# A decoder layer whose ternary feed-forward weights are made in the first batch instead of before the feed-forward

## The reference

```python
x = x + attn(layernorm(x))                  # 16 heads of 32, rotary, causal; w_qkv, w_o
x = x + ssm(ctx, z=layernorm(x))            # state-space scan, 16 states for each of 512 channels
x = x + ffn(layernorm(x))                   # below

def ternarize_weights(w):
    gamma = mean(abs(w))                    # one number for the whole matrix
    return sign(round(w / (gamma + EPS))) * gamma
def bitlinear(x, w):                        # forward value
    return einsum(absmax_quant(layer_norm(x)), ternarize_weights(w))
ffn = bitlinear(gelu(bitlinear(x, w_fc)), w_proj)     # 512 -> 2048 -> 512
```

## Time and profile before

| | us |
|---|---|
| median of 3 runs (lowest, highest) | 1058.46 (1055.85, 1059.35) |
| the profiled execution's own time | 1058.11 |
| its span | 1056.3 |
| PE busy | 949.3 |
| DVE busy | 853.2 |
| ACT busy | 764.9 |
| POOL busy | 616.9 |

### The profile page before, as it was taken

How to read it: one execution, slowest core, us unless ns; L and a number is a source line. 1 busy time by engine, 2 the same in 40 slices (tenths; PEclk the granted TensorE clock), 3 DMA queues, 4 the chain that set the end, 5 groups by cost and what they waited for, 6 DMA issues and landing times.

```text
span 1056.3 us, 18159 instructions
## 1 busy us (share of the span) xinstructions
PE 949.3 (90%) x5848; PEld 641.1 (61%) x5848; DVE 853.2 (81%) x1151; ACT 764.9 (72%) x1478; POOL 616.9 (58%) x439
## 2 busy tenths in 40 slices
PE   6989998899988999979889997667889999999997
PEld 5466666668755567765555876556755555555544
DVE  5797878986999987898999686998998889885431
ACT  4776867646787775677898669958279989996431
POOL 1387496555545778444658872345667768985410
PEclk9999999999999999978999998989989999999999
DMA  5356265265326544342336555224325565646553
GB/s 168 101 171 187 84 188 172 86 193 155 116 81 217 159 140 136 110 131 60 110 111 205 194 169 192 61 90 138 97 71 116 110 125 120 120 95 140 99 93 69
DMA packets 142812, 136.84 MB, mean 130 GB/s; under 512 B 92336, under 2 KB 96688, under 8 KB 141696
## 3 DMA queue, kind: packets, MB, share of 16 engines
q1 hardware_dynamic: 142720, 135.68, 46.1%
HBM read 90.42 MB, written 24.25 MB: 109 GB/s over the span
## 4 chain that ended last, share of the span: by engine, by line
PE 57%; DVE 20%; issue 9%; ACT 7%; POOL 4%; DMA 2%; SPq 0%; DVEq 0%; ACTq 0%; POOLq 0%
PE ps L1679 10%; PE ps L1748 8%; PE ps L1805 8%; PE ps L1795 8%; DVE hb L1825 6%; PE ps L1692 5%; PE ps L1760 5%; DVE y_acc L1847 4%; PE ps L1722 4%; DVE m_col L1922 2%; PE ps L1734 2%; POOL hb L1295 2%; ACT p_q L1526 2%; PE ps L1622 2%; DVE du L1879 1%
## 5 line engine op out<-in xcount | busy, mean ns | idle before, releaser
L1295 POOL TENSOR_TENSOR hb<-du,b_bc 128x1024 f32<-128x1024 f32 (+1 forms) x160 | 311.5, 1967 | 160.3 <-PE ps L1748 146.6
L1825 DVE TENSOR_TENSOR_SCAN hb<-ps,hb 128x1024 f32<-128x1024 f32 (+1 forms) x128 | 257.2, 2013 | 15.9 <-ACT ps L1415 13.5
L1415 ACT ACTIVATE ps<-delta,a_neg 128x511 f32<-128x511 f32 (+2 forms) x320 | 179.2, 597 | 72.6 <-DVE hb L1825 71.3
L1847 DVE SCALAR_TENSOR_TENSOR y_acc<-ps,ct,y_acc 128x512 f32<-128x512 f32 x256 | 182.0, 742 | 39.0 <-PE ps L1748 38.3
L1748 PE MATMUL ps<-ident,hb 128*128 128x128 f32 x1088 | 157.1, 288 | 35.1 <-DVE hb L1825 15.5
L1748 PEld LDWEIGHTS ps<-ident,hb 128*128 128x128 f32 x1088 | 129.5, 148 | 66.1 <-issue 17.8
L1526 ACT ACTIVATE p_q<-ps,m_col 128x512 f32<-128x512 f32 (+3 forms) x256 | 131.6, 530 | 26.4 <-DVE m_col L1922 22.0
L1795 PE MATMUL ps<-t_fc,xt 128*128 128x512 f16 x512 | 119.4, 387 | 3.3 <-DMA xt<-xs 3.3
L1679 PE MATMUL ps<-xn_t,w_ring 128*128 128x512 f32 x256 | 118.7, 608 | 2.2 <-DVE y_acc L1969 1.0
L1805 PE MATMUL ps<-t_pr,ht 128*128 128x512 f16 x512 | 114.7, 383 | 3.7 <-DMA ht<-hs 3.3
L1542 ACT ACTIVATE p_t<-ps 128x512 f32<-128x512 f32 x160 | 86.5, 603 | 30.6 <-PE ps L1722 30.2
(11 more groups left out here) (141 smaller groups left out, 1559.5 us busy)
## 6 DMA issues: line engine op xcount, KB each, us to landing
w_ring<-in_w_attn SPq DMA_DIRECT2D x32, 512.0 KB, 3.7
qk_d<-hl SPq DMA_DIRECT2D x64, 256.0 KB
q_st<-qk_d SPq DMA_DIRECT2D x128, 128.0 KB, 2.9
...
k_st<-qk_d SPq DMA_DIRECT2D x128, 64.0 KB, 2.3
...
raw_fc<-in_w_fc SPq DMA_DIRECT2D x4, 1024.0 KB, 9.5
```

The lines of the kernel that those rows point to most:

```text
L1295: nc.gpsimd.tensor_tensor(piece_of(e, hi, lo).rearrange("p (a n) -> p a n", a=2), du[b % 2][:, 2 * h:2 * h + 2, lo:hi], b_bc[:, i % BC_RIN ...
L1415: ins = nc.scalar.activation(factors(j, hi, lo)[:, (hi - lo) * m + start:(hi - lo) * (m + 1)], delta[b % 2][:, et, lo + start:hi], ACT.Exp ...
L1825: v.tensor_tensor_scan(h, d, h, 0.0, ALU.mult, ALU.add).then_inc(scan_done, 1)
L1847: v.scalar_tensor_tensor(out=y, in0=bank(kind, r, tb), scalar=ct[:, b % 2, tb, n:n + 1], in1=y, op0=ALU.mult, op1=ALU.add).then_inc(y_free ...
```

## The change

Four things change. The ternary weights are made from the start of the program on, in pieces of 1024 columns through a ring of two: 16 pieces are loaded and summed on ACT, then the same 16 are loaded again, compared on DVE, and stored as float16 in device memory (`t_d`). When the last batch's projections are over, two DMAs load them into `t_fc` and `t_pr`. The ring lies in the second half of `y_acc`, and the comparison's outputs over `gate`, so the second batch's first sum waits for all 16 comparisons and the first `gate` for all stores. The buffers of the feed-forward are laid out anew: `h_sb` lies over the attention's q and k and waits only for the last scores. `XF`, the ring of feed-forward inputs, goes from 7 to 5. And the tables of wished times are replaced by one entry for each state, slot and tile, with new weights, new durations in `follows()`, and `PATIENCE` 0.18 for 0.3.

```diff
-XF = 7
+XF = 5
+RAW = 1024
+RAWS = KD * FF // RAW
+SUMS = 2 * RAWS
-PATIENCE = 0.3
+PATIENCE = 0.18
-STATE = {'exp': [-3.1, 2.9], 'dbu': [-19.1, -2.9], 'scan': [0, 6], 'ht': [7.6, 8.8, 10, 11.2]}
+WEIGHTS = {'fwload': [-82.44, -84.05, -41.76, -59.47, -57.03, -35.38, -62.34, -32.59, -22.52, -61.3, 25.5, -20.65, -24.85,
...
     elif kind == "fwload":
-        w, n = a
-        yield "sp", 6, [act("v", B - 1, 1, 1), sp("lo", B - 1, 3), pool("delta", B - 1, ET - 1)] if w == 0 else \
-            [pe("s", SLOTS - 1, 4) if n < 2 else (act("exp", 2 * DS * (B - 1) - 1), pool("dbu", 2 * DS * (B - 1) - 1))[n - 2]]
+        k, = a
+        yield "sp", 3.0, [act("wsum", k - 2) if k - 2 < SUMS else dve("tern", k - 2 - SUMS)] if k >= 2 else []
...
-        yield "dve", 0.8, [pe(*item)] + ([act("e", p - 1, n)] if p else [])
+        yield "dve", 0.66 if n in (1, 4) else 0.6, [pe(*item)] + ([act("e", p - 1, n)] if p else [])
...
-        yield "act", 1.3, [dve("s", *a)] + ([pe("t", a[0] - 1, 4)] if a[0] else [])
+        yield "act", 0.67 if n in (0, 3) else 0.91, [dve("s", *a)] + ([pe("t", a[0] - 1, 4)] if a[0] else [])
...
     elif kind == "tern":
-        w, n = a
-        yield "dve", 3.7, [dve("wtot", w)]
+        k, = a
+        yield "dve", 1.85, [dve("wtot", k // RAWS), sp("fwload", SUMS + k), dve("delta", 0, ET - 1)] + ([sp("tstore", k - 2)] if k >= 2 else [])
...
+            us *= slow.get(engine, 1.0)
...
-            over[engine, item] = at + us + 0.2
+            over[engine, item] = at + us + settle[engine]
...
+        base[0] = stack_at
+        h_sb = sb("h_sb", [P, 2, FF])
...
+        base[0] = y_acc_at + 4 * LT * DM
+        raw = sb("raw", [P, 2, RAW])
+        base[0] = gate_at
+        low = sb("low", [P, 2, RAW], BF16)
+        tern = sb("tern", [P, 2, RAW], F16)
...
                 elif kind == "fwload":
+                    k, = a
+                    w, c = divmod(k % SUMS, RAWS)
+                    if k >= 2:
+                        if k - 2 < SUMS:
+                            sp.wait_ge(wsum_ready, k - 1)
+                        else:
+                            sp.wait_ge(tern_done, k - 1 - SUMS)
+                    sp.dma_start(raw[:, k % 2, :], t_in[("w_fc", "w_pr")[w]][:, RAW * c:RAW * c + RAW])\
+                        .then_inc(raw_in[k % 2], 16)
+                elif kind == "tstore":
+                    k, = a
+                    w, c = divmod(k, RAWS)
+                    sp.wait_ge(tern_done, k + 1)
+                    sp.dma_start(t_d[w, :, RAW * c:RAW * c + RAW], tern[:, k % 2, :]).then_inc(t_stored[k % 2], 16)
...
                 elif kind == "tern":
+                    k, = a
+                    w = k // RAWS
+                    if k == 0:
+                        delta_made(dve, 0, ET - 1)
+                    if k >= 2:
+                        dve.wait_ge(t_stored[k % 2], 16 * (k // 2))
+                    dve.wait_ge(raw_in[k % 2], 16 * ((SUMS + k) // 2 + 1))
+                    v.tensor_scalar(low[:, k % 2, :], raw[:, k % 2, :], nthr[:, w:w + 1], None, ALU.is_lt).then_inc(is_low, 1)
+                    dve.wait_ge(is_low, k + 1)
+                    v.scalar_tensor_tensor(out=tern[:, k % 2, :], in0=raw[:, k % 2, :], scalar=thr[:, w:w + 1],
+                                           in1=low[:, k % 2, :], op0=ALU.is_gt, op1=ALU.subtract).then_inc(tern_done, 1)
```

More of the change, by code:

```diff
@@ L323 @@
-PACE = {'slot': 18.4, 'ffn': 597.2, 'tile': 15.5, 'tail': 822.6, 'tail_step': 13.6, 'tail_load': -18.7}
+WEIGHT = {'pe': {'ln1b': 1.9,
+        'inproj': -9.5,
+        'xproj': 2.0,
+        'ct': 9.0,
+        'dt': 0.5,
+        'rot': 2.0,
+        'v': 20.2,
+        's': 5.5,
+        't': 3.0,
+        'pv': 61.8,
+        'rz': -4.7,
+        'wo': 17.2,
+        'ht': -2.9,
+        'gt': 4.0,
+        'wtot': 70.8,
+        'xt': 60.6,
+        'fc': -16.2,
+        'ht_ffn': -21.9,
+        'proj': 2.4},
+ 'act': {'carry': -7.8,
+         'exp': -2.8,
+         'skip': -16.1,
+         'ht': -31.6,
+         'ln1b': 47.1,
+         'inproj': -34.1,
+         'silu': 24.7,
+         'xproj': -35.9,
+         'ct': -36.2,
+         'dt': 20.5,
+         'hi': -3.2,
+         'v': 41.1,
+         'e': 1.7,
+         't': -6.7,
+         'pv': 9.8,
+         'rz': -1.0,
+         'gate': -20.6,
+         'xt': -9.7,
+         'ht_ffn': -15.4,
+         'fc': 0.5,
+         'wsum': -23.8,
+         'hn': -21.1},
+ 'dve': {'scan': 0.1,
+         'ht': 7.1,
+         'ln1a': 10.9,
+         'ln1b': 12.1,
+         'inproj': 19.4,
+         'delta': -9.0,
+         'rot': -28.5,
+         's': 0.1,
+         'rz': -9.2,
+         'pv': -28.5,
+         'wo': -4.7,
+         'ln2a': 17.7,
+         'ln2b': 30.4,
+         'gt': -0.9,
+         'wtot': -13.4,
+         'tern': -7.8,
+         'xa': 25.0,
+         'xc': -3.8,
+         'xt': -8.9,
+         'ht_ffn': -19.6,
+         'fc': -23.6,
+         'hstat': 19.2,
+         'hn': 0.9,
+         'hq': -18.5,
+         'proj': -11.1},
+ 'pool': {'delta': 22.8,
+          'dbu': 0.6,
+          'du': -4.9,
+          'lo': 13.3,
+          'xadd': -27.3,
+          'ln1a': -11.3,
+          'ln2a': 2.0,
+          'xa': 5.0,
+          'xc': 15.2,
+          'hstat': -19.7},
+ 'sp': {'xload': 9.4,
+        'cload': 17.5,
+        'wload': -8.9,
+        'lo': -17.3,
+        'xproj': -45.1,
+        'bcload': 18.0,
+        'stack': -10.5,
+        'resid': -24.2,
+        'x2store': 0.6,
+        'fwload': 24.6,
+        'fxload': -27.2,
+        'proj': -13.0}}
@@ L326, in schedule @@
+TILE = {'fxload': [-66.44],
+ 'xa': [-69.82],
+ 'xc': [-40.92],
+ 'xt': [-35.82],
+ 'fc': [-9.26, -30.81, -10.14, -14.5],
+ 'hstat': [-77.43],
+ 'hn': [16.74, 6.58],
+ 'ht_ffn': [-12.97, -15.2],
+ 'proj': [18.32]}
+FIRST_TILE = {'xa': [17.57], 'xc': [-19.46]}
+SWITCH = 17.35
+PATIENCE = 0.18
 def schedule():
@@ L1233, in _ @@
                         sp.wait_ge(hl_stored, 64 * 4 * B)
[L1234 to L1239 removed]
+                    for n in range(2):
+                        sp.wait_ge(t_stored[n], 16 * (w + 1) * RAWS // 2)
+                    dst = (t_fc, t_pr)[w][:].rearrange("p a n -> p (a n)")
+                    sp.dma_start(dst, t_d[w]).then_inc(tw_in[w], 16)
                 elif kind == "fxload":
@@ L1784, in _ @@
                     w, = a
[L1785 to L1786 removed]
+                    pe.wait_ge(wsum_ready, RAWS * (w + 1))
+                    nc.tensor.matmul(bank(kind, *a)[:, 0:RAWS], ones[:], w_sum[:, w, :], start=True, stop=True)\
                         .then_inc(y_full, 1)
```

623 lines of the change are left out of this document (272 added, 351 removed), and 9 rows, old and new, of tables (ATTN_END, SKIP).

## The result

| | before | after |
|---|---|---|
| median (lowest, highest), us | 1058.9 (1055.85, 1060.19) | 1005.28 (1004.94, 1006.11) |
| span of the profiled execution | 1056.3 | 1004.2 |
| first `fc` matmul | 766.7 | 731.3 |
| from the first `fc` to the last scan transposes | 190 | 211.5 |
| from the last scan transposes to the end | 99 | 61.4 |

What follows compares the result with a forecast made beforehand. DVE was taken to bound the kernel up to the first `fc`, PE and ACT up to the last scan transposes, PE and the last tile's chain after: 734 + 208 + 67 = 1009 us of span, 1011 us timed; range 984 to 1046.

Steps and rivals of the forecast that it cites:

- First `fc` at 734: Start to first `fc` matmul: 53 us, then 612.5 us of DVE work at a chosen 0.90; 734 against 767.
- Contention, 7 us: Comparisons in the first batches: running beside POOL lengthens them, adding 7 us of DVE work; bounds 0 and 34.
- rival 2: Comparisons: POOL and DVE block each other in all 16, 34 in place of 7 us of DVE; 1041 us, chance 0.08.
- Both are places where DVE has work waiting. So moving them gains no DVE time by itself: Ahead of first `fc`: comparisons move from 656.6 us and later into the first batches, without DVE gain by itself.
- DVE sets the pace: Up to first `fc`: DVE, busy 621.5 of 714 us (0.87) after the first 53, limits; PE's 0.88 is partly fills.
- The rate rises because fills are fewer and durations nearer to the trace: Ahead of first `fc`: DVE's rate goes above 0.87, to 0.90; fills fall from 399 to 209, planner durations match the trace.
- Stretch 2: First `fc` to last scan transposes: PE 201.5 and ACT 195.3 us of work; 208 us (203 to 214), 17 longer.
- Stretch 3: Last scan transposes to the end: PE work 58.1, idle 6.5 kept, 2.5 added; 67 us (64 to 74) against 98.3.
- The two new waits: Tail: possible waits at the last two tiles' first multiplications, 12 us after the gate, and the last `proj`; 2.5 us added.
- Rival 3: Weight reloads through SP: each of 16 comparisons waits 4.3 us, DVE loses 69 us; 1080 us, chance 0.07.
- The granted clock: Whole kernel: stays at or above the present 0.94 in every stretch although 372 fills go, because matmuls stand closer.
- rival 4: No change: DVE stays at 0.87 before first `fc`, PE's share falls to 0.87 after it; 1058 us, chance 0.05.

## Why the prediction was right, and where its reasons were not

The forecast was 1011 us, the time 1005. The sum was right stretch by stretch in the work that it counted. What carried the gain ahead of the first `fc` was DVE's rate, and that was not derived: 0.90 was taken as the middle between 0.87 and 0.93. Four kernels with the same early weights ran at 0.80 to 0.91, so that it came to 0.911 here was in part luck.

- **First `fc` at 734; it came at 731.** The sum held: DVE's work ahead of the mark was 30.4 + 617.9 = 648.3 us against 645.5 (comparisons 40.9 against 36, the rest 607.4 against 609.6), and the rate 0.911 against the chosen 0.90.
- **Contention, 7 us.** The comparisons took 40.9 us against 29 + 7; above their shortest forms they lost 9.9, and the two shortest halves of a piece cost 0.27 us more than the piece whole, 2 us for the eight. The mechanism was right, and the size near. The rule of the Trainium skill that was weighed there (SBUF — State Buffer, "SBUF: two separate sides": a lock held for the whole instruction) agrees in that single instructions are long; as a price for every step beside POOL, these rows don't bear it out. Waits in all 16 (rival 2, 34 us) aren't seen: the median of the second step is its minimum, 1285 against 1283 ns, and only five of these 16 are long, up to 2.17 us.
- **"Both are places where DVE has work waiting. So moving them gains no DVE time by itself".** This is the step that failed, though the number didn't. Moving the weights is worth 31 us under the new orders and costs 70 under the old. In the first batches DVE had idle time to take them: from 116 to 590 it does the same other work in the kernel after (438.0 - 40.8 = 397.2 us) as with late weights and new orders (398.9). Up to the first `fc` the other work is 648.3 - 40.9 = 607 us against 625 less its 21 of comparisons, 604, and the kernel after is there 15 us earlier with 23 us more in its list. The prediction read the rate of the whole stretch and of two windows of it, took the missing tenth as crossings of waits, and let the moved work run at the same rate as all other. But the comparisons are not what is dear late: made short there, they give 6 us. The other 25 stay open.
- **"DVE sets the pace".** Half right. 46.4 us more of its work cost 46.5, but 23 us less gave 4. So DVE work has no one price there: adding costs all of its length, removing gives a fifth.
- **The rate rises because fills are fewer and durations nearer to the trace.** The second half is shown: with new tables, old durations lose 98 us, but the DMA line's factor alone loses 86 when it is undone, an edit that the prediction left uncosted; the durations that it named, of maxima and exponentials, are in the rest. The number of fills was read as a sign of the plan's fit; as matmuls they matter little, since without any the time is 2.5 us longer, within the uncertainty.
- **Stretch 2, 208 us; it was 211.5.** PE 202.8 against 201.5 of work, ACT 199.9 against 195.3. Both are above 0.93, as said. The prediction took it as the price of moved work alone. With late weights and new orders the stretch takes 231, with 8 us more of PE's work in it, so ready weights are worth up to 20 us here, which it did not see.
- **Stretch 3, 67 us; it was 61.4.** PE's work was as counted (57.9 against 58.1). The idle time was mis-sized: 6.5 was kept and 2.5 added, 3.5 was measured. The two new waits didn't come, and the old one went.
- **Rival 3, the reload loop:** dead, 0.4 us of waiting for `raw`. It had named the right place for a loss, though by another way: not the transfer but the plan's belief about it.
- **Table loads at 1.28 us, without a drain behind them:** right. In the kernel after one begins at 733.96 and takes 1.28 us, and the next instruction of ACT starts at 735.26.
- **The granted clock "should not fall below the present 0.94 in any stretch":** wrong. It is 0.90 from 590 to 731 (0.93 before, but 0.90 from 400 to 480), where DVE and PE both have gaps (122.8 and 120.3 of 141), with and without fills. The mark came where the sum had it all the same.
- **The chances.** Those listed for faster, 0.56 + 0.17 + 0.08 + 0.07 and a third of rival 4, make 0.90, not 0.88; nothing else hangs on it.
